# Last batch of a fused attention and feed-forward block: the first half's attention moved one slot ahead, its rows added by VectorE and stored through ScalarE's queue

## The reference

```python
xn = layernorm(x)
q, k, v = split(xn @ qkv_w + qkv_b)           # 16 heads of 16 channels
q, k = l2norm(q), l2norm(k)
kv = einsum('bhnd,bhne->bhde', k, v)          # over all 1024 tokens of a batch
attn = einsum('bhnd,bhde->bhne', q, kv) @ proj_w + proj_b
ffn = relu(xn @ W1 + b1) @ W2 + b2
out = x + attn + ffn
```

## Time and profile before

| | us |
|---|---|
| median of 3 timed runs | 581.59 |
| time of the profiled execution | 583.1 |
| its span | 581.4 |
| TensorE busy | 564.9 (97%) |
| VectorE busy | 413.9 (71%) |
| ScalarE busy | 283.5 (49%) |
| GpSimd busy | 122.1 (21%) |

### The profile page before, as it was taken

One profiled execution on the slowest core, in us unless ns is written; L12 is line 12 of the kernel. 1 busy time (PEld: TensorE's weight loads), 2 busy tenths in 40 slices (PEclk: granted clock), 3 DMA queues, 4 the chain that ended last, 5 costly groups with the idle time before them and its releaser, 6 DMA issues.

```text
span 581.4 us, 8936 instructions
## 1 busy us (share of the span) xinstructions
PE 564.9 (97%) x2720; PEld 479.3 (82%) x2720; DVE 413.9 (71%) x804; ACT 283.5 (49%) x516; POOL 122.1 (21%) x150
## 2 busy tenths in 40 slices
PE   8899899999999999999999999999999999999993
PEld 6688688888888888888888888888888888888893
DVE  5886878768687677867678595776778677773743
ACT  2675463455635555355633646445543656334320
POOL 1335320420233010520205202231015202050012
PEclk9989899999999999999999999999999999999997
DMA  8313235145332535135451353425343252505043
GB/s 296 102 37 72 41 83 97 25 86 97 84 76 57 114 50 124 21 85 93 86 93 20 85 93 84 79 36 109 68 106 42 50 95 45 99 14 95 13 97 73
DMA packets 141398, 45.36 MB, mean 78 GB/s; under 512 B 133314, under 2 KB 136386, under 8 KB 141380
## 3 DMA queue, kind: packets, MB, share of 16 engines
q1 hardware_dynamic: 141376, 45.13, 38.3%
q10 hardware_dynamic: 4, 0.01, 0.0%
HBM read 20.98 MB, written 8.39 MB: 51 GB/s over the span
## 4 chain that ended last, share of the span: by engine, by line
PE 91%; SPq 3%; DVE 2%; issue 1%; POOL 1%; DMA 0%; ACT 0%; POOLq 0%; DVEq 0%
PE o_bank L974 11%; PE o_bank L975 11%; PE o_bank L976 11%; PE w_bank L976 10%; PE w_bank L974 10%; PE w_bank L975 10%; PE v_bank L974 6%; PE v_bank L975 6%; PE v_bank L976 6%; SPq L301 3%; PE g_bank L974 3%; PE g_bank L976 3%; PE g_bank L975 3%; PE w_bank L1143 1%; PE kv_bank L1095 1%
## 5 line engine op out<-in xcount | busy, mean ns | idle before, releaser
L801 DVE SCALAR_TENSOR_TENSOR h_lo<-w_bank,h_hi 128x512 fp32r<-128x512 f32 x128 | 87.4, 683 | 40.4 <-ACT h_hi L519 38.9
L519 ACT ACTIVATE h_hi<-w_bank 128x512 fp32r<-128x512 f32 x128 | 76.3, 596 | 78.9 <-PE w_bank L976 77.0
L976 PE MATMUL w_bank<-xT_hi,w_lo 128*128 128x512 f32 x254 | 100.1, 394 | 0.0
L974 PE MATMUL w_bank<-xT_hi,w_hi 128*128 128x512 f32 x254 | 100.1, 394 | 0.0
L975 PE MATMUL w_bank<-xT_lo,w_hi 128*128 128x512 f32 x254 | 100.0, 394 | 0.0
L365 POOL TENSOR_TENSOR xn_lo<-xn,xn_hi 128x256 fp32r<-128x256 f32 x60 | 44.5, 741 | 249.8 <-ACT xn_hi L456 246.2
L974 PE MATMUL o_bank<-h_hi,w_hi 128*128 128x512 f32 x240 | 94.9, 396 | 0.0
L975 PE MATMUL o_bank<-h_lo,w_hi 128*128 128x512 f32 x240 | 94.8, 395 | 0.0
L976 PE MATMUL o_bank<-h_hi,w_lo 128*128 128x512 f32 x240 | 94.6, 394 | 0.0
L380 POOL TENSOR_TENSOR y_sb<-y_sb,y_rows 128x256 f32<-128x256 f32 x60 | 56.0, 937 | 132.0 <-DVE y_rows L840 128.4
L497 ACT ACTIVATE qk_sq<-v_bank 128x512 f32<-128x512 f32 x64 | 38.3, 598 | 84.6 <-PE v_bank L976 84.6
(11 more groups left out here) (180 smaller groups left out, 985.8 us busy)
## 6 DMA issues: line engine op xcount, KB each, us to landing
qT_lo<-blocks SPq DMA_DIRECT2D x256, 32.0 KB, 1.9
out<-y_sb SPq DMA_DIRECT2D x62, 128.0 KB, 2.7
x_sb<-x SPq DMA_DIRECT2D x15, 512.0 KB, 3.9
y_sb<-x SPq DMA_DIRECT2D x60, 128.0 KB, 3.4
xT_raw<-blocks SPq DMA_DIRECT2D x224, 32.0 KB, 1.9
y_sb<-w SPq DMA_DIRECT2D x4, 256.0 KB, 4.8
w_raw<-w SPq DMA_DIRECT2D x1, 768.0 KB, 9.0
x_sb<-x SPq DMA_DIRECT2D x2, 256.0 KB, 3.0
```

The source lines that it names most:

```text
L519: nc.scalar.activation(h_hi[:, j % RING, :], w_bank[j % 2][:], ACT.Relu).then_inc(h_done, 1)
L801: nc.vector.scalar_tensor_tensor(h_lo[:, r, :], w_bank[j % 2][:], 0.0, h_hi[:, r, :].bitcast(F32), ALU.max, ALU.subtract).then_inc(h_lo_do ...
L974: nc.tensor.matmul(to, left[0], right[0], start=first, stop=False, skip_group_check=shared)
L976: return nc.tensor.matmul(to, left[1], right[0], start=False, stop=last, skip_group_check=shared)
```

## The change

It touches the last batch only, apart from the place of some waits in the code of TensorE's `attend`. Four things are done: TensorE does the first half's attention between the seventh and the eighth `ffn_down` of the last half; VectorE adds the first half's rows in one instruction of 128x1024, ahead of `add_last`; ScalarE's queue issues the four stores of the first half; and the x rows of both halves are loaded in the batch's first half, ahead of the last `move_q`. GpSimd's bias add is in its program right behind that load.

```diff
@@ SyncE: half, end
-                else:
+                if u == (0 if last else 1):
                     if isinstance(b, int) and b == 0:
                         sp.wait_ge(w1_ready, PARTS)
                     for loaded_half in range(2):
                         load_y(b, loaded_half, last)
...
-                store_y(b, 0)
                 rows = out_halves[2 * b + 1]
@@ GpSimd: half, end
                 if not last:
                     split_xn(s + 2, u)
-
-            def end(b, last):
-                if last:
+                elif u == 0:
                     pool.wait_ge(bias_out_ready, 1)
                     add_last_bias(b)
-                add_rows(b, 0)
+
+            def end(b, last):
                 if not last:
+                    add_rows(b, 0)
                     add_rows(b, 1)
@@ ScalarE: end
+                    return
+                act.wait_ge(y_done, TILES * 2 * b + 1)
+                for q in range(GROUPS):
+                    rows = slice(q * BLOCK, (q + 1) * BLOCK)
+                    act.dma_start(out_blocked[2 * b][q], by_block(y_sb[rows, 0])).then_inc(stored[0], 16)
@@ VectorE
+            def add_rows(b):
+
+                dve.wait_ge(y_loaded[0], 16 * GROUPS * (b + 1))
+                dve.wait_ge(yT_spread, KC * (2 * b + 1))
+                nc.vector.tensor_tensor(y_sb[:, 0], y_sb[:, 0], y_rows[:, 0], ALU.add).then_inc(y_done, 1)
...
                 if last:
+                    add_rows(b)
                     add_last(b)
                     return
@@ TensorE: attend, half, end
+            def attend(b, u, banks):
                 wait(pe, m_lo_done, b + 1)
+                wait(pe, qT_lo_done, 2 * b + u + 1)
+                for k in range(KC):
+                    for g in range(KC):
+                        done = product(banks[k][:], (m_hi[:, g, channels(k)], m_lo[:, g, channels(k)]),
+                                       (qT_hi[:, u, g, :], qT_lo[:, u, g, :]), g == 0 and u == 0, g == KC - 1,
+                                       shared=u == 1)
+                    done.then_inc(o_ready, 1)
...
                     ffn_down(s, b, u, j, last)
+                    if j == 6 and not ahead:
+                        pe.wait_ge(h_lo_done, JC * (s + 1))
+                        attend(b, 0, w_bank)
...
             def end(b, last):
-                attend(b, last)
+                if last:
+                    attend_last(b)
+                    return
+                wait(pe, qk_copied, TILES * (2 * b + 3))
+                attend(b, 0, v_bank)
+                attend(b, 1, o_bank)
```

More of the change, by code:

```diff
@@ L1107, in project, with attend_last @@
                 done.then_inc(m_ready, 1)
-            def attend(b, last):
+            def attend(b, u, banks):
                 wait(pe, m_lo_done, b + 1)
[L1111 to L1130, removed]
+                wait(pe, qT_lo_done, 2 * b + u + 1)
[5 more added lines that the diff above has]
+                    done.then_inc(o_ready, 1)
+            def attend_last(b):
+                wait(pe, qT_lo_done, 2 * b + 2)
                 for t in range(TILES):
```

## The result

| | before | after |
|---|---|---|
| median, runs taken in turns on one chip | 582.14 (8 runs, 580.99 to 583.09) | 579.61 (8 runs, 577.49 to 581.54) |
| time of the profiled execution | 583.1 | 581.54 |
| its span | 581.4 | 579.7 |

The ratio is 0.9955 with a 95% interval of 0.9939 to 0.9972: faster. The forecast was 578.3 us, within 577.0 to 579.5, and a ratio of 578.3 / 581.59 = 0.9943. That ratio lies in the interval; the time, 579.61, is 1.3 above the forecast and 0.1 outside the range. The medians are 2.53 apart; in us the interval is a gain of 1.6 to 3.6, which holds the forecast's 3.3 too.

What follows compares the result with a forecast made beforehand. The prediction took the tail as bound by the DMA engines, started late by the first half's chain. Attention -1.20, row-add engine -2.01 and denser tail -0.1 made -3.3: 581.59 to 578.3 us, range 577.0 to 579.5.

Steps and rivals of the forecast that it cites:

- the swap: TensorE, last batch: first half's attention moved ahead of the last down slot ends 1.20 us earlier.
- the m_lo wait: TensorE, start of the moved attention: new stall of 0.24 us for the weights' low part from VectorE.
- the drain: Final stores: DMA engines take 5.18 us for 1.05 MB, then 0.92 to the end; 0.1 us gain taken.
- The early loads: x rows loaded a half sooner: bias add near 541.3 holds VectorE's divide 1.6 us, TensorE doesn't stall; cost 0 to 0.5.
- The last line of the sum: End of the forecast: 3.3 us taken off 581.59, the median of three timed runs, giving 578.3 us.
- -2.01 for the engine: First half's row adds on VectorE for GpSimd: 2.01 of the 3.21 us by which the store is released earlier.
- By that rule this part of the change gives nothing of its own.: First half's stores through ScalarE's queue: issuers share 16 DMA engines, more issuers only save issue time; no gain.
- Faster draining by two queues: Rival, final stores: two queues drain faster than one, ending at 576.7 to 577.2 us; chance 15%.
- Small costs together: Rival: early bias add holds VectorE at the wrong moment, or ScalarE issues at twice SP's time; 578.9 to 579.6 us; 15%.
- The long m_lo wait: Rival, TensorE before the moved attention: m_lo comes 1.2 us later, the swap gives nothing; 579.6 us; 3%.
- an end that isn't the first half's: Rival, kernel's end: the stores' completion has a cost that doesn't move; 580.5 to 582 us; 4%.
- blocked loads: Rival, SP's queue: x loads wait for batch 6's stores and delay the moves of q; slower, 583 us from 21 slip; 3%.

Runs made afterwards that it cites:

- the repeats: Both kernels, before and after, run again unchanged, against the kernel before: before 582.68 us, ratio 1.0013; after 578.94 us, ratio 0.9959.
- the pair with the extra matmuls: Both kernels with identity matmuls in three waits of the opening, against the kernel before: before 581.29 us, ratio 0.9986; after 577.79 us, ratio 0.9941.
- the pair's: VectorE's row adds and ScalarE's store queue, both taken back at once from the changed kernel: 580.15 us, tail 16.90 for 14.72.

## Why the prediction was wrong

By its own steps:

- *What bounds the kernel; the swap; the m_lo wait; the row add; the drain.* Right, each within 0.1 us (table above). The tail is 3.32 shorter in the profiled pair, 3.42 in the repeats, 3.37 in the pair with the extra matmuls; forecast 3.3.
- *The early loads.* Right: bias add at 543.03, which less the shift of 1.61 is 541.4, divide held for 1.6 us, TensorE not touched. The 0.8 that the prediction put on a bias add left beside qT_lo is not tested: it depends on who comes first, and the one run that could show it had VectorE first.
- *The last line of the sum, "581.59 - 3.3 = 578.3", and the range around it.* **This is the step that failed.** The 3.3 was right; the 581.59 it was taken from is a median of three runs, and such a median isn't a fixed number here. The same kernel stands at 582.14, 582.22 and 582.68 in later sets and at 581.3 in the last, since its single times lie in groups and the median goes with how many fall in which. In the result's own eight runs it is 582.14, 0.55 above the 581.59. The other 0.77 of the 1.3 is that the medians are 2.53 apart and not 3.3: after's eight times lie in three groups (577.49 to 577.96, 579.43 to 579.94, 581.27 and 581.54), before's in two. Group by group the middle values are 581.41 and 577.84, 583.05 and 579.79, which is 3.6 and 3.3 apart; only after drew a third group, which the kernel before has too when it is run more often (584.61 to 585.12 in three of 27). The range was made from the costs of the change alone and held nothing for this, though one of three runs and the profiled execution itself (583.1, with 581.59 beside it) had shown 1.5 us of it. The medians of before, less 3.3, go from 578.0 to 579.4, and the two of after are 578.94 and 579.61: a range had to hold all that. Where the groups come from is shown in the traces: the 12 identity passes at the start (1.8 us), and TensorE's clock at the waits near 26, 64 and 70 us (up to 3). Which of them each single time had is not on record, and what makes the 12 passes slow or fast stays open.
- *"-2.01 for the engine".* Right as a difference of two issues (3.13 - 1.17 = 1.96), wrong as a worth: it is the pair's. The sum came out right because the prediction took all edits together, from the first issue to the end.
- *"By that rule this part of the change gives nothing of its own."* Wrong for the kernel before. That rule of the Trainium skill (DMA: Bandwidth & Descriptors, Issuing engines are not separate DMA queues), that more issuers only save issue time, doesn't cover the 2.15 us that the second queue alone gave, and the measurement decides. I asked how fast two queues drain and not who stands behind whom; yet I had written in the first part that the last half's rows waited over 4 us on SP's queue. The queue gives 0.26 with the new adds and 2.15 in the kernel before.
- *Rivals.* Faster draining by two queues: no, 60.9% for 63.2% of the same 7.4 us. Small costs together: the divide was held, and the fourth of ScalarE's issues took long, but neither cost time that shows. The long m_lo wait, an end that isn't the first half's, and blocked loads: none came.

## What to carry to other kernels

When two streams of output end in the same DMA engines, ask when these last have work, not when each stream is ready: two edits that fill the same hole are worth their gain once, and a store that is ready behind one that isn't wastes it all. A change of 3 us at the end of a kernel whose opening scatters by 4 us must be read from a common point near the end; the time itself needs a range that holds the scatter, and a base of more than three runs. Look at the single times before trusting a median: where they lie in groups, compare group with group. An overlap that depends on 0.4 us between two engines is no constant price; give it both values. Matmuls that only keep TensorE busy are work in its queue: ahead of something urgent they can be late themselves.

## What was not expected of the hardware

- In the tail of after, the four issues of ScalarE took 2.88 us and the two of SP 1.91, for 2.25 and 0.93 where the queues didn't meet in time (second queue alone). The last issue of each is the long one, 1.37 and 1.38 us, while the DMA engines are at seven to nine tenths. The longest on a single queue is 0.81 in the kernel before and 0.95 with the stores on SP. No run shows what holds it, and it held up nothing here that shows, as both queues were at their ends.
- Of two instructions that read both operands from SBUF on VectorE and GpSimd, the later one stands for the rest of the earlier one, less 0.13 to 0.15 us, in either direction (fourteen meetings).
- TensorE at full clock in one stretch of the opening ran into a longer wait (2.05 us for 0.30) and did the next stretch at 0.50 to 0.65, and so ended 1.6 us behind the execution that had been slow first.
- Twelve passes of identity matmuls at 7 us took 2.93 us in five executions and 1.60 in nine, with the granted clock shown as 1.00 in both, and moved the whole kernel by 1.8.
